# Spline tables about anchors at every fourth knot, with two additions moved to accumulating DMAs

## The reference

```
x: (32, 64, 56, 56) float32
out = relu(bn1(conv3x3(x, sign(w1))))           # bn over batch and pixels
x   = relu(bn2(conv3x3(out, sign(w2))) + x)
u   = (clip(a*x + b, -1.5, 1.5) + 1) * 0.5 * 31  # a, b per channel; 32 knots
i, t = floor(u), u - floor(u)
spline = sum_n alpha_table[clip(i-1+n, 0, 31)] * B_n(t)     # cubic B-spline, 8 curves
out = id_gain*x + sum_r spline_r * mix[c, r] + bias
```

## Time and profile before

| | |
|---|---|
| median of three runs | 1305.97 us (1305.14 to 1306.96) |
| the profiled execution | 1308.54 us, span 1306.8 us |
| PE busy | 1251.1 us, 96% of the span |
| DVE busy | 1004.3 us, 77% |
| ACT busy | 898.5 us, 69% |
| POOL busy | 62.8 us, 5% |
| DMA | 235.94 MB, mean 181 GB/s |
| spline stage, first matmul to last instruction | from 444.17 us to the end |

### The profile page before, as it was taken

How to read it: one execution, slowest core, us unless ns; L and a number is a source line. 1 busy time by engine, 2 the same in 40 slices (tenths; PEclk the granted TensorE clock), 3 DMA queues, 4 the chain that set the end, 5 groups by cost and what they waited for, 6 DMA issues and landing times.

```text
span 1306.8 us, 63386 instructions
## 1 busy us (share of the span) xinstructions
PE 1251.1 (96%) x29706; PEld 904.4 (69%) x29706; DVE 1004.3 (77%) x907; ACT 898.5 (69%) x359; POOL 62.8 (5%) x156
## 2 busy tenths in 40 slices
PE   7999997999997499999999999999999999999998
PEld 5688886888886266656666666666666666668997
DVE  5666565856667688878888888888888888888866
ACT  4445446777774488668886788778886888678860
POOL 6000000570000000000000000000000000000000
PEclk9999998999999699999999999999999999999999
DMA  6676656576676555455665556545654455455411
GB/s 240 233 289 255 255 228 253 221 282 255 259 288 242 155 185 155 136 126 151 176 162 138 149 157 174 147 126 157 184 157 129 150 181 158 138 150 158 126 46 52
DMA packets 53654, 235.94 MB, mean 181 GB/s; under 512 B 15824, under 2 KB 15824, under 8 KB 45392
## 3 DMA queue, kind: packets, MB, share of 16 engines
q1 hardware_dynamic: 52528, 230.88, 55.1%
q10 hardware_dynamic: 928, 1.90, 0.5%
HBM read 104.29 MB, written 77.07 MB: 139 GB/s over the span
## 4 chain that ended last, share of the span: by engine, by line
PE 65%; DVE 1%; ACTq 0%; issue 0%; ACT 0%; DVEq 0%
PE tab L1102 65%; ACTq L912 0%; DVE lin L1058 0%; DVE poly L1054 0%; DVE zbuf L964 0%; DVE lin L958 0%; DVE poly L1030 0%; DVE poly L1036 0%; DVE mask L994 0%; ACT zbuf L896 0%; ACT cell L904 0%; DVE lin L970 0%; DVEq L1029 0%; DVEq L957 0%
## 5 line engine op out<-in xcount | busy, mean ns | idle before, releaser
L1102 PE MATMUL tab<-mask,diag 128*32 128x392 bf16 x20480 | 853.7, 330 | 26.0 <-DVE mask L994 23.4
L1102 PEld LDWEIGHTS tab<-mask,diag 128*32 128x32 f16 x20480 | 582.4, 97 | 297.0 <-DVE mask L994 23.5
L926 ACT ACTIVATE mask<-cell,thr 128x6272 bf16<-128x6272 bf16 x93 | 509.3, 5508 | 2.2 <-PE tab L1102 2.0
L1030 DVE SCALAR_TENSOR_TENSOR poly<-tab,first,poly 128x1568 f32<-128x1568 f32 x92 | 170.3, 1851 | 105.8 <-PE tab L1102 102.5
L698 PE MATMUL acc<-band_split,w 64*64 64x392 f16 x4608 | 198.6, 331 | 8.8 <-ACT band_split L361 7.2
L698 PE MATMUL acc<-split,w 64*64 64x392 f16 x4608 | 197.3, 331 | 10.0 <-DVE w L456 9.1
L403 ACT ACTIVATE yout<-acc 128x1568 f32<-128x1568 f32 x64 | 94.2, 1472 | 162.0 <-PE acc L698 140.8
L698 PEld LDWEIGHTS acc<-band_split,w 64*64 64x64 f16 x4608 | 165.6, 107 | 41.5 <-issue 13.1
L698 PEld LDWEIGHTS acc<-split,w 64*64 64x64 f16 x4608 | 155.1, 107 | 51.5 <-issue 10.6
L896 ACT ACTIVATE zbuf<-lin,cst 128x1568 f32<-128x1568 f32 x32 | 54.3, 1697 | 181.7 <-DVE lin L958 175.9
L513 DVE BATCH_NORM_STATS2 stats<-yout 128x392 f32 (+1 forms) x240 | 118.2, 555 | 62.7 <-ACT yout L403 61.8
(11 more groups left out here) (115 smaller groups left out, 396.2 us busy)
## 6 DMA issues: line engine op xcount, KB each, us to landing
y_scratch<-yout SPq DMA_DIRECT2D x32, 1568.0 KB, 6.2
cell<-cell SPq DMA_DIRECT2D x496, 98.0 KB, 3.7
xin<-y_scratch SPq DMA_DIRECT2D x16, 1568.0 KB, 9.0
zbuf<-y_scratch SPq DMA_DIRECT2D x32, 784.0 KB, 4.7
lin<-in_x SPq DMA_DIRECT2D x32, 784.0 KB, 9.0
out<-lin SPq DMA_DIRECT2D x31, 784.0 KB, 5.0
xin<-in_x SPq DMA_DIRECT2D x15, 1568.0 KB, 9.4
cell<-cell ACTq DMA_DIRECT2D x16, 98.0 KB, 3.4
```

The costliest lines, as they stand in the source:

```text
L926: act.activation(mask[b % 2][q][:, :, :], cell4[b % 2][:, :, :], ACT.Sign, bias=thr[:, q:q + 1]).then_inc(sign_mask_ready, 1)
L1030: dve.scalar_tensor_tensor(out=quarters(poly), in0=summed(i, b, t), scalar=base(i, b, t), in1=quarters(poly), op0=ALU.add, op1=ALU.add).th ...
L1102: mm = pe.matmul(tab[(b + t) % 2][j * GROUP:(j + 1) * GROUP, sub, 0:SUB], keep["diag"][part][:, j % 2, t, q, :], mask[b % 2][q][:, j, sub ...
```

## The change

The coefficients are now taken about an anchor at every fourth knot (8 thresholds for value, slope and bend, instead of 16), and about every second knot for third differences. With d = u - anchor (|d| up to 2) a chunk computes

`value + slope*d + d^2*(bend + near*|d|) + far * relu(|d|-1)^3`

- Tables NEAR and FAR have 16 thresholds (4 quads); SQ, LIN and VAL have 8, which are quads 0 and 1, the "edges". A chunk has 448 matmuls instead of 640.
- Masks: DVE makes two (the "middle" quads 2 and 3, single buffered, after table FAR of the chunk before), ACT two (the edges).
- ACT gets four new passes per chunk over 128 x 1568: `scale` (lin = scale*y), `far_distance` (relu(|d|-1)), `far_square`, `distance_square`; `sides` becomes `distance`.
- `total` leaves DVE for chunks from 2 on: ACT scales y into `lin` and a DMA issued by POOL adds x (784 KB) into it. The far part, computed by DVE in the tile `far`, is also added into `lin` by such a DMA (`add_far`, SBUF to SBUF, 784 KB).
- DVE's combination is `near_cube`, `far_cube`, `far_part`, add SQ, `near_part`, `slope`, `add_slope`, add VAL, `finish`.
- SP's body does `load` (y alone) before `store`. PE's order of quads is 2, 3, 0, 1. `coefficients` and `steps`, which build the small tables during the convolutions, are rewritten; the prologue on DVE makes the offsets of chunk 1 too.

```diff
-T_ABS, T_CUBE, T_SQ, T_LIN, T_VAL = range(TABLES)
-SIGN_QUADS = (1, 2, 3)
-VECTOR_QUADS = (0,)
+T_NEAR, T_FAR, T_SQ, T_LIN, T_VAL = range(TABLES)
+EDGE_QUADS = (0, 1)
+MIDDLE_QUADS = (2, 3)
+QUAD_ORDER = MIDDLE_QUADS + EDGE_QUADS
+QUADS_OF = (QUAD_ORDER, QUAD_ORDER, EDGE_QUADS, EDGE_QUADS, EDGE_QUADS)
...
+        @block.gpsimd
+        def _(pool):
+            def add_x(c):
+                pool.wait_ge(scaled, c - 1)
+                pool.dma_start(lin[c % BUFS][:, :], x[c // 2][:, (c % 2) * CHUNK:(c % 2 + 1) * CHUNK],
+                               accum_op=ALU.add).then_inc(x_added, 16)
+            def add_far(c):
+                pool.wait_ge(far_part_ready, 2 * c + 2)
+                pool.dma_start(lin[c % BUFS][:, :], far[:, :], accum_op=ALU.add).then_inc(far_added, 16)
+            add_x(2)
+            for c in range(CHUNKS):
+                add_far(c)
+                if c + 3 < CHUNKS:
+                    add_x(c + 3)
...
+            def scale(i, b):                         # ACT
+                act.wait_ge(y_loaded[b % 2], 16 * (2 * i + b // 2 + 1))
+                wait_past(act, stored[b % BUFS], 16 * (i + b // BUFS))
+                act.activation(lin[b % BUFS][:, :], place[b % 2][:, :], ACT.Identity,
+                               scale=cc(BN2_S)).then_inc(scaled, 1)
             def position(i, b):
-                act.wait_ge(sum_ready, BUFS * i + b + 1)
+                    act.wait_ge(x_added, 16 * (c - 1))      # chunks from 2 on
...
+            def distance(i, b):
+                act.wait_ge(offset_ready, c + 1)
+                wait_past(act, whole, c - 1)
+                act.activation(poly[b % 2][:, :], offset[b % 2][:, :], ACT.Abs, scale=1 / POINT).then_inc(dist_ready, 1)
+            def far_distance(i, b):
+                act.wait_ge(dist_ready, c + 1)
+                wait_past(act, far_added, 16 * c)
+                act.activation(far[:, :], poly[b % 2][:, :], ACT.Relu, bias=cc(MINUS_1)).then_inc(far_ready, 1)
+            def far_square(i, b):
+                wait_past(act, slope_ready, 2 * c)
+                act.activation(far_sq[:, :], far[:, :], ACT.Square).then_inc(far_sq_ready, 1)
+            def distance_square(i, b):
+                wait_past(act, near_ready, 2 * c)
+                act.activation(dist_sq[:, :], offset[b % 2][:, :], ACT.Square, scale=1 / POINT).then_inc(dist_sq_ready, 1)
...
             def body(i, b, n):                       # ACT
+                far_distance(i, b)
                 if after:
                     position(i, b + 2)
+                far_square(i, b)
                 if after:
                     cells(i, b + 2)
+                distance_square(i, b)
                 if following:
+                    distance(i, b + 1)
+                    edge(i, b + 1, EDGE_QUADS[0])
+                if third:
+                    scale(i, b + 3)
+                if following:
+                    edge(i, b + 1, EDGE_QUADS[1])
...
             def body(i, b, n):                       # DVE
                 if previous:
+                    add_table(i, b - 1, T_VAL, slope_ready, 2 * (BUFS * i + b - 1) + 2)
                     finish(i, b - 1)                 # waits for far_added
                 if after:
                     fixed(i, b + 2)
+                near_cube(i, b)                      # poly = (NEAR + base) * |d|, waits for far_ready
+                if after:
                     linear(i, b + 2)
+                far_cube(i, b)                       # far = (FAR + base) * far
+                far_part(i, b)                       # far = far * AMP * far_sq
+                if following:
+                    for q in MIDDLE_QUADS:
+                        middle(i, b + 1, q)          # waits for table FAR of chunk c
+                add_table(i, b, T_SQ, table_used, used(i, b, T_NEAR))
+                near_part(i, b)                      # poly = poly * dist_sq
+                slope(i, b)                          # far_sq = (LIN + base) * offset
+                add_slope(i, b)
+                if after:
+                    offsets(i, b + 2)
```

More of the change, by code:

```diff
@@ L538, in coefficients @@
             def coefficients():
[L540 to L558, removed]
+                def knots(t, first, count, by):
+                    return t[:, :, first:first + by * (count - 1) + 1:by]
@@ new lines, in coefficients @@
+                link(dve.memset(bend[:, :, :], 0.0), chain)
+                link(dve.tensor_tensor(bend[:, :, 0:KNOTS], ctl[:, :, 0:KNOTS], ctl[:, :, 2:KNOTS + 2], ALU.add), chain)
+                link(dve.scalar_tensor_tensor(out=bend[:, :, 0:KNOTS], in0=ctl[:, :, 1:KNOTS + 1], scalar=-2.0,
+                                              in1=bend[:, :, 0:KNOTS], op0=ALU.mult, op1=ALU.add), chain)
+                for start, first, count in ((0, 0, ANCHORS), (1, 4, ANCHORS - 1)):
+                    at = slice(start, CENTRES, 2)
+                    before, here, after = (knots(ctl, first + n, count, 4) for n in range(3))
+                    value, slope, square = (coef[:, :, t, at] for t in (T_VAL, T_LIN, T_SQ))
+                    link(dve.tensor_tensor(value, before, after, ALU.add), chain)
+                    link(dve.scalar_tensor_tensor(out=value, in0=here, scalar=4.0, in1=value, op0=ALU.mult,
+                                                  op1=ALU.add), chain)
+                    link(dve.tensor_tensor(slope, after, before, ALU.subtract), chain)
+                    link(dve.tensor_copy(square, knots(bend, first, count, 4)), chain)
+                    link(dve.tensor_tensor(coef[:, :, T_NEAR, at], knots(bend, 1 + 2 * start, count, 4),
+                                           square, ALU.subtract), chain)
@@ new lines, in add_table, with near_part @@
+            def add_table(i, b, t, made, count):
+                dve.wait_ge(made, count)
+                dve.wait_ge(table_ready, used(i, b, t))
+                dve.scalar_tensor_tensor(out=quarters(poly[b % 2]), in0=summed(i, b, t), scalar=base(i, b, t),
+                                         in1=quarters(poly[b % 2]), op0=ALU.add, op1=ALU.add).then_inc(table_used, 1)
+            def near_part(i, b):
+                c = BUFS * i + b
+                dve.wait_ge(table_used, used(i, b, T_SQ))
+                dve.wait_ge(dist_sq_ready, c + 1)
+                dve.tensor_tensor(poly[b % 2][:, :], poly[b % 2][:, :], dist_sq[:, :], ALU.mult).then_inc(near_ready, 2)
```

255 lines of the change are left out of this document (134 added, 121 removed).

## The result

The changed kernel takes 1261.8 us (median of 4 runs, 1260.0 to 1266.3) against 1305.56 us: a ratio of 0.9678 (0.966 to 0.9695), 3.2% faster where 6.6% was forecast. The profiled execution takes 1260.0 us, with a span of 1258.2 us.

A forecast was written before the change was run, and what follows sets the result against it. PE, busy 96%, bounds the kernel before; after, the PSUM loop at 23.4 us plus 0.3 for POOL, times 31, gives 734.7, with 485.8 for start and end: 1220 us forecast, range 1204 to 1310.

The forecast's parts named there:

- DVE's sum: DVE's operations in one chunk of the new body, added up from row distances: 22.8 us, as much as before.
- Start and end: Before and after the 31 periods: near_cube(0) at 464.2 us, 12 us lost; then 2.8, 11.0 and 7.8, sum 485.8.
- L: Time from the end of ACT's scale to the landing of the x DMA, taken as 8.5 us.
- I take 8.5 us: 7.1 and 1.4 for those copies.: x DMA's landing time: 7.1 us with twice the engine time for an addition, 1.4 for the copies' last quarter.
- PSUM loop: NEAR waits until slope has read LIN from the shared buffer; NEAR, FAR and DVE's operations to slope: 23.4 us a chunk.
- rival 5: PE, idle a few us in each loop, gets the lower clock; at half clock PSUM loop 34 us; within slower's 0.20.
- x loop: From ACT's position through scale and the x DMA to the next position: 14.4 us plus 8.5 landing, 22.9 a chunk.
- POOL held up: DVE can shut out POOL's DMA issue: 0.3 us a chunk taken; by the skill the far DMA starts 3.5 us later.
- Rival 1: The x DMA sets the pace, landing after 10.5 us: 24.9 us a chunk, 1259 us; chance 0.28 together with rival 3.
- Rival 2: The x DMA lands after 13.2 us, so chunks take 27.6 and the kernel 1345 us; nearly all of slower's 0.20.
- Rival 3: POOL shut out, each far DMA waits for the masks, say 14 us: 24.9 a chunk, 1259; 0.28 with rival 1.
- Rival 4: Square forces ACT table loads of 1.3 us, four a chunk: ACT 26.6 us, about no change, 1306; no own chance.

The follow-up runs named there:

- e10: Changed kernel with the x DMA adding only half of the columns and DVE's add SQ and slope moved ahead of the middle masks: 1201.7 us.
- e2: Changed kernel with the x part undone: SP loads x by a plain DMA and DVE adds scaled y: 1253.5 us, ratio to before 0.9616.
- e4: Changed kernel with POOL's x DMA overwriting lin instead of adding, same bytes, scaled y left out: 1256.8 us.
- e3: Changed kernel with the x DMA adding only 784 of 1568 columns from chunk 2 on: 1240.1 us.
- e8: Changed kernel with the far DMA cut to 8 of 1568 columns, far part left out: 1240.4 us.
- e11: Changed kernel with the sixteen cell copies carrying half of the columns from chunk 2 on: 1242.0 us.
- e15: Changed kernel with the x DMA adding half of the columns, plus 160 short unused PE matmuls a chunk ahead of table LIN: 1237.1 us.
- e9: Changed kernel with DVE's add SQ and slope moved ahead of the two middle masks: 1256.0 us, ratio to before 0.963.
- e1: Changed kernel with ACT's scale before the first edge mask, so the x DMA may start earlier: 1276.5 us, ratio to before 0.9799.
- filler runs: 160 short unused PE matmuls a chunk added to the changed kernel, with x added in half of the columns (1237.1 us) or in all (1269.1 us).
- e5: Changed kernel with only DVE's add SQ moved ahead of the middle masks, slope left in place: 1282.8 us.
- e16: Changed kernel with ACT's position later, DVE's add SQ and slope before the middle masks, far DMA cut to 8 columns: 1227.3 us.

## Why the prediction missed

Point by point:

- *PE is the bound and loses 8 us of work a chunk; DVE's sum 22.8, ACT's 21.4.* Right. e10 runs its chunks at 22.9, DVE's sum; near_part, which I had to bound, is 1.79 long. ("Nine combining operations stand for ten" miscounts: there are nine in both kernels, the tenth was `total`. The sum doesn't use it.)
- *Start and end.* Right, to 1.1 us at the start and 0.1 at the end. The 12 us lost at the start came as forecast, and e2, without that wait, got 8 of them back.
- *An addition costs the DMA engines two transfers.* Right. The last far addition, which stands alone, takes 41.3% of the 16 engines from 1240 to 1250 us, 4.1 us for the 4.2 estimated; in the mean of all 62 it is 4.3 (the software queue's 21.0% of 1258.2 us). The page of the Trainium skill that puts the cost of a reducing collective in its two source reads (Collectives: The Full Stack, "The bandwidth ceiling: the fold count and why AG ≠ RS ≠ AR") agrees with this as far as the time of an addition that stands alone goes. It doesn't decide L: e4 without the addition lands only half a us sooner.
- **First failed step: "I take 8.5 us: 7.1 and 1.4 for those copies."** The mechanism was there, the size was off. From scale's end to position's start it is 10.6. The copies and the far DMA, not the copies' tail alone, run beside x, and the engines are all but full (0.89 to 1.00) for some 16 us of each 25. With 14.4 on ACT that is 25.0 for the 22.9 forecast, so this loop doesn't stay "just under the other": it is the one that ends last in most chunks. Cost: 0.6 us a chunk, 24.9 where e3, e8 and e11 have 24.3.
- **Second failed step: the PSUM loop's "23.4 us. PE idles in it some 4.7 us a chunk, but never long."** It idles once a chunk for 4 us, and table VAL runs behind it at 0.50. I had the clock as rival 5, but as a catastrophe at half speed throughout, and put no part of it into the sum. Reckoned with VAL at 4.2 us, as many chunks of e8 have it: from far_cube 9.0 to SQ read, 4.2, NEAR and FAR 10.7, with hand-offs 24.0, as those chunks measure; the mean is 24.3, since in some VAL takes up to 5.4. Cost: 0.7 us for the clock (e15 against e3), and 0.2 for hand-offs, since e15's chunks take 23.6 at full clock for the 23.4 of the sum.
- 23.4 + 0.9 + 0.6 = 24.9. The split between the two steps depends on which is cured first: the PSUM loop alone holds 24.3 (e3, e8, e11), the x loop alone 24.75 (e9), both together 24.88. The 0.3 us for POOL against DVE weren't needed: the masks are 1.85 us long, for 1.84 before.
- *POOL held up.* Small, but there: the far DMA's issue takes 1.59 us beside a mask and 0.86 beside none (e9), and in e9 the x DMA, which there meets the masks, takes 1.86 and ends at 873.18, 0.1 us after the second mask (873.07). The Trainium skill (SBUF — State Buffer, "SBUF: two separate sides") has POOL shut out for the whole of such an operation, and the rows agree: it is held to the end of the one mask that runs. What was wrong is the price that I worked out from it: 0.7 to 1.0 us, the rest of one mask, and not the 3.5 of both.
- *Rival 1* named the result (L = 10.5, 24.9, 1259). Its time was right and its cause half right: with L cured alone (e8) only 21 of the 38 us come off, so that its sum met the measured time so closely is in part luck. *Rival 2* would have needed L over 12.3; e1 had 14.1 and still 25.35 us, since there scale stood earlier. *Rival 3*, the far DMA, hardly binds: ACT waits 4.5 us for it in all. *Rival 4*: no table load stands in the stage. *Rival 5* had the right cause and the wrong size.

Open: what the "issue" stalls of the filler runs are, and what decides whether the clock falls after a gap of 2.2 us.

## What to carry to other kernels

When the bound is taken off one engine, work out every loop of waits that is left, and take the landing time of a transfer as something that the rest of the traffic sets: a DMA started earlier beside others can land so much later that time is lost (e1). Two binders of nearly the same length hide each other, so an edit that seems worthless alone (e9: 0.13 us a chunk) can be worth 1.3 us on top of another. An engine that was 96% busy and is then 84% busy may also become slower, if its gaps come in one piece: here 4.4 us in one piece brought the clock to 0.50 behind it, and e9's order, with no gap over 2.3 us from 480 to 1180 us, kept 1.00. What follows a long gap should not be on the loop: with the same 4 us in front of VAL (changed kernel) and in front of NEAR (e5) the periods are 24.9 and 25.6.

## What the runs showed of the hardware that was not expected

- One 784 KB addition landed after 5.9 us where it stood alone (the last far addition), and after 14.1 us in e1's traffic (median of x, DMA share 0.84).
- Dropping the addition and keeping the bytes changed landing from 10.3 to 9.8 us, and the engines' time for such a transfer by 1.2 us (e4).
- The granted clock was 0.50 in the 6 us after a gap of 4.4 us, though PE was busy 83% of the stage's time. Through e9's gaps of up to 2.3 us (480 to 1180 us) it stayed at 1.00. In e16 the same gap of 2.24 us came with 0.72 in the window from 866 to 872 us and with 1.00 in that from 890 to 896.
- POOL's issue of a DMA took 0.86 us, and 1.59 to 1.86 beside a mask of DVE (e9, the changed kernel).
